# A fused attention and expert kernel: the keys interleaved like the queries, and the next batch's projections put behind its transposes

## What is computed

```python
x = L0_attn_x                                   # 16 sequences, 512 tokens, 128 features
h = _layernorm(x) * (1 + ca) + sa               # sa, ca, ga, sb, cb, gb: rows per sequence
# attention with 16 heads of 8 dimensions and 32 random features per head
q = feature_map(split(h @ Wq.T + bq), orf)      # (exp(y @ orf.T / 8**0.25 - |y|**2 / (2*sqrt(8))) + EPS) / sqrt(32)
k = feature_map(split(h @ Wk.T + bk), orf)
v = split(h @ Wv.T + bv)
kv, ksum = einsum('nlm,nld->nmd', k, v), sum(k, axis=1)
out = (q @ kv) / (q @ ksum)
x = x + ga * (out @ Wo.T + bo)
h = _layernorm(x) * (1 + cb) + sb
# eight experts 128 -> 512 -> 128; every token goes to the one with the largest gate value
x = x + gb * _L0_ffn_ref(h, gate_W, gate_b, W1, b1, W2, b2)
```

## Time and profile before

| what | value |
|---|---|
| median of three runs | 381.62 us |
| span of the profiled execution | 360.6 us |
| TensorE matmul busy | 338.8 us, 94% |
| VectorE, ScalarE, GpSimd busy | 75%, 74%, 59% |
| first stage, q features of batch 1 to those of batch 15 | 29.5 to 204.2 us |
| second stage | from about 211 us to the end |
| granted TensorE clock, mean | 0.998 |

### The profile page before, as it was taken

The page is one execution under the profiler, slowest core; times in us unless marked ns, Lnnn a source line. Parts: engine busy times, 40 slices in busy tenths (PEclk is TensorE's granted clock), DMA queues, the critical chain, the costliest instruction groups (busy, mean ns, idle before and its releaser), DMA issues.

```text
span 360.6 us, 13729 instructions
## 1 busy us (share of the span) xinstructions
PE 338.8 (94%) x4823; PEld 263.9 (73%) x4823; DVE 271.2 (75%) x1104; ACT 265.1 (74%) x644; POOL 213.2 (59%) x262
## 2 busy tenths in 40 slices
PE   6899999899988999998999999999999999999994
PEld 5445765566465566646665669999989999999993
DVE  3456997898879789878887978887677676666653
ACT  2688988799878888977888756676656667666761
POOL 3142386776667757857854618846767455545554
PEclk9999999999999999999999999999999999999999
DMA  7174656774566547444432467445657665545410
GB/s 233 50 253 166 210 184 221 259 243 160 177 227 205 176 167 230 163 132 156 153 133 100 149 163 227 142 118 150 194 161 269 209 184 147 147 128 135 137 38 12
DMA packets 40211, 60.47 MB, mean 168 GB/s; under 512 B 5426, under 2 KB 28086, under 8 KB 40016
## 3 DMA queue, kind: packets, MB, share of 16 engines
q1 hardware_dynamic: 33776, 42.54, 39.9%
q0 software_dynamic: 6368, 17.05, 12.5%
HBM read 28.63 MB, written 19.34 MB: 133 GB/s over the span
## 4 chain that ended last, share of the span: by engine, by line
PE 60%; ACT 15%; DMA 10%; DVE 6%; issue 5%; POOL 1%; SPq 1%; DVEq 1%; POOLq 0%; ACTq 0%
PE ps_proj L1350 16%; PE ps_feat L1337 9%; DMA qmix<-qsqs 9%; PE ps_proj L1132 6%; PE ps_den_gate L1337 4%; PE ps_proj L1182 4%; PE ps_kv L1337 4%; ACT qf L627 3%; ACT qvals L606 2%; ACT shared L588 2%; PE ps_kv L1198 2%; PE ps_out L1330 2%; ACT den L656 2%; ACT shared L581 2%; ACT kvm L600 2%
## 5 line engine op out<-in xcount | busy, mean ns | idle before, releaser
L545 POOL DMA_INDIRECT out<-kf,modb x71 | 70.1, 987 | 52.4 <-DVE kf L1060 47.0
L507 POOL DMA_INDIRECT experts_lists<-pay,slot x64 | 65.9, 1030 | 43.4 <-DVE slot L893 29.5
L1350 PE MATMUL ps_proj<-w2sb,qf 128*128 x568 | 75.0, 275 | 0.4 <-ACT qf L690 0.4
L1350 PEld LDWEIGHTS ps_proj<-w2sb,qf 128*128 128x128 f32 x568 | 68.9, 192 | 0.6 <-issue 0.6
L681 ACT ACTIVATE xT<-ps_out 128x128 f32<-128x128 f32 x71 | 19.7, 277 | 44.8 <-PE ps_out L1330 44.1
L1055 DVE TENSOR_TENSOR kf<-ps_proj,firsts_sb 128x128 f32<-128x128 f32 x71 | 20.7, 291 | 34.6 <-PE ps_proj L1350 22.6
L690 ACT ACTIVATE qf<-ps_feat,shared 128x128 f32<-128x128 f32 x144 | 40.9, 374 | 0.0
L1337 PE MATMUL ps_feat<-xT,shared 128*128 128x128 f32 x288 | 38.8, 277 | 1.5 <-issue 0.9
L1337 PEld LDWEIGHTS ps_feat<-xT,shared 128*128 128x128 f32 x288 | 35.0, 192 | 2.8 <-issue 1.7
L1132 PE MATMUL ps_proj<-shared,wsb 128*128 128x512 f32 x62 | 33.3, 620 | 1.0 <-ACT shared L581 0.4
L977 DVE COPY shared<-firsts_sb 128x516 f32 x71 | 31.4, 442 | 1.6 <-issue 1.5
(11 more groups left out here) (189 smaller groups left out, 890.3 us busy)
## 6 DMA issues: line engine op xcount, KB each, us to landing
modb<-experts_lists SPq DMA_DIRECT2D x71, 196.0 KB, 2.8
xall<-in_x SPq DMA_DIRECT2D x16, 256.0 KB, 3.0
pay<-modb SPq DMA_DIRECT2D x16, 256.0 KB, 3.0
qmix<-qvals SPq DMA_DIRECT2D x30, 128.0 KB
qmix<-qsqs SPq DMA_DIRECT2D x30, 128.0 KB
modb<-modulation_rows SPq DMA_DIRECT2D x4, 768.0 KB, 5.2
firsts_sb<-in_firsts SPq DMA_DIRECT2D x8, 322.0 KB, 4.2
w2sb<-in_w SPq DMA_DIRECT2D x8, 256.0 KB
```

The lines of the kernel that those rows point to most:

```text
L507: g_.indirect_dma_start(out=lists, in_=pay[b.home][:, t, :], in_offset=None, out_offset=bass.IndirectOffsetOnAxis(ap=slot[b.home][:, t:t + ...
L545: g_.indirect_dma_start(out=rows_out, in_=yb[u], in_offset=None, out_offset=bass.IndirectOffsetOnAxis(ap=token, axis=0), bounds_check=last ...
L1350: ins = mm(Y[u % 2][:, 0:D], g[u % R4][:, c * P:(c + 1) * P], w2sb[:, bass.ds(e * DFF + c * D, D)], start=(c == 0), stop=(c == FC - 1))
```

## The change

The key weights get the column order that the query weights have. kvals and ksqs are copied by four DMAs per batch into a new tile kmix (mix_k, ahead of mix_q in SyncE's order), from batch 1 on. The k features of batches 1 to 15 are then one product from kmix with the moving operand feat_q, 64 columns wide, for each of 4 token tiles, 2 halves and 4 row groups: 32 matmuls as before, each with 32 rows and 128 stationary columns. Batch 0 keeps the two-product form with constants in the new order.

On TensorE the k projection of b+1 now stands right behind the transposes that it needs, the q projection right behind the kv product, and the transposes of h2 ahead of the k features. On ScalarE the copies of k come before the copy of kv, and the squares of q right behind the values of q.

```diff
+            def mix_k(v):
+                sp.wait_ge(s_kst, 2 * v + 1)
+                for n in range(2):
+                    sp.dma_start(kmix[n::2, n, :], kvals[n::2, :]).then_inc(s_kmix, 16)
+                sp.wait_ge(s_kst, 2 * v + 2)
+                for n in range(2):
+                    sp.dma_start(kmix[1 - n::2, n, :], ksqs[n::2, :]).then_inc(s_kmix, 16)
             for v in range(1, B):
+                mix_k(v)
                 mix_q(v)
...
                 q_pair(b, 1, first)
-                kvm_copy(b)
                 if not last:
                     k_values(b + 1)
                     k_squares(b + 1)
+                kvm_copy(b)
+                if not last:
                     q_values(b + 1)
+                    q_squares(b + 1)
                 act.wait_ge(s_den, b.v + 1)
...
-                if not last:
-                    q_squares(b + 1)
                 if b.v + 2 < B:
                     normalise1(b + 2)
...
+            def k_features(b):
+                pe.wait_ge(s_kmix, 64 * b.v)
+                pe.wait_ge(s_fq, 1)
+                pe.wait_ge(s_eps, b.v)
+                pe.wait_ge(s_qst, b.v + 1)
+                pe.wait_ge(s_exp, NC * b.v)
+                for t in range(LT):
+                    for n in range(2):
+                        for c in range(NC):
+                            at = slice(c * CW, (c + 1) * CW)
+                            ins = mm(QB[c][:, t * P + n * HP:t * P + (n + 1) * HP], kmix[at, n, t * P:(t + 1) * P],
+                                     feat_q[at, n, :], start=True, stop=True)
...
-                k_features(b, first)
                 if not first and not second:
                     transpose_h2(b + -2, first=third)
+                if first:
+                    first_k_features(b)
+                else:
+                    k_features(b)
...
+                if not last:
+                    project(b + 1, 0)
                 kv_product(b, first)
                 if not last:
-                    project(b + 1, 0)
+                    project(b + 1, 1)
...
                 kv_transpose(b, first)
-                if not last:
-                    project(b + 1, 1)
```

More of the change, by code:

```diff
@@ L80 @@
 R_NORMQ = R_ORFQ + P
-R_NORMV = R_NORMQ + P
-R_END = R_NORMV + P
+R_END = R_NORMQ + P
 class Batch:
@@ L142, in build @@
         feat_q = sb("feat_q", [P, 2, P // 2])
-        feat_v = sb("feat_v", [P, P])
         bv_cols = sb("bv_cols", [P, D])
@@ L172, in build @@
         qsqs = sb("qsqs", [P, L])
+        kmix = sb("kmix", [P, 2, L])
         qmix = sb("qmix", [P, 2, L])
@@ L281, in build @@
         s_qsq = sem("q_squares_ready")
+        s_kmix = sem("k_mix_ready")
         s_qmix = sem("q_mix_ready")
@@ L1141, in v_project, with first_k_features @@
                 ins.then_inc(s_proj, 1)
[L1143 to L1149, removed]
+            def first_k_features(b):
+                pe.wait_ge(s_kst, 2)
                 for t in range(LT):
@@ L1159, in k_features @@
                             ins.then_inc(s_feat, 1)
+            def k_features(b):
[10 more added lines that the diff above has]
+                                     feat_q[at, n, :], start=True, stop=True)
+                            if t == LT - 1 and n == 1:
+                                ins.then_inc(s_feat, 1)
             def q_features(b, first=False):
@@ L1172, in q_features @@
                         at = slice(c * CW, (c + 1) * CW)
-                        mm(QB0[c][:, :], feat_v[at, :], qvals[at, :], start=True, stop=False)
+                        mm(QB0[c][:, :], feat_w[at, :], qvals[at, :], start=True, stop=False)
                     for c in Q_ORDER:
                         at = slice(c * CW, (c + 1) * CW)
-                        mm(QB0[c][:, :], rsb[at, R_NORMV:R_NORMV + P], qsqs[at, :], start=False, stop=True).then_inc(s_feat, 1)
+                        mm(QB0[c][:, :], norm_w[at, :], qsqs[at, :], start=False, stop=True).then_inc(s_feat, 1)
                     return
@@ L1304, in batch @@
                 kv_transpose(b, first)
-                if not last:
-                    project(b + 1, 1)
-                else:
+                if last:
                     keep_busy(14, H)
@@ L1415, in _constants @@
     for r in range(P):
-        head = r // DH % (CW // DH)
-        c[r, C_NORM + head * M:C_NORM + (head + 1) * M] = -1.0 / (2.0 * DH ** 0.5)
+        at = C_NORM + (r % 2) * HP + r % CW // 2 // DH * M
+        c[r, at:at + M] = -1.0 / (2.0 * DH ** 0.5)
     c[:, C_PREF:C_PREF + E] = np.arange(E, 0, -1)
@@ L1437 @@
     w[:, W_O:W_O + D] = a(L0_attn_Wo).T
-    orf = a(L0_attn_orf).T
-    for head in range(NH):
-        at = W_ORF + head % (CW // DH) * M
-        w[head * DH:(head + 1) * DH, at:at + M] = orf
     w[:, W_GATE:W_GATE + E] = a(L0_ffn_gate_W)
@@ L1454 @@
                 rows[square, R_NORMQ + n * HP + j * M:R_NORMQ + n * HP + (j + 1) * M] = -1.0 / (2.0 * DH ** 0.5)
-                rows[value, R_NORMV + n * HP + j * M:R_NORMV + n * HP + (j + 1) * M] = -1.0 / (2.0 * DH ** 0.5)
-    w[:, W_Q:W_Q + P] = w[:, W_Q:W_Q + P][:, source]
-    w[:, W_BIAS + 1] = w[source, W_BIAS + 1]
+    for n in range(2):
+        w[:, n * P:(n + 1) * P] = w[:, n * P:(n + 1) * P][:, source]
+        w[:, W_BIAS + n] = w[source, W_BIAS + n]
+    w[:, W_ORF:W_ORF + P] = rows[:, R_ORFQ:R_ORFQ + P]
     firsts = np.zeros((P, E, WB), np.float32)
```

2 lines of the change are left out of this document (removed).

## The result

The changed kernel takes **434.0 us** (median of five runs, 428.39 to 435.57), the kernel before 383.65 beside it (five runs, 381.19 to 385.29). The ratio is 1.128, with a 95% interval of 1.119 to 1.138. So the medians lie 50 us apart. The forecast was 427, 45 us more, in a range of 410 to 438.

A forecast was written before the change was run, and what follows sets the result against it. TensorE was taken as full in the first stage, every wait a hole. Fourteen periods of 15.41 us add 41.0, batch 1 adds 4: +45 on the span 360.6, plus 21.0 outside it, gives 427 us; range 410 to 438.

The forecast's parts named there:

- First projection, +1.06: TensorE idles 1.12 us for hT at Q (start of a batch's q features)+2.93; kv product follows: +1.06 us per period.
- Second projection, +0.97: Before the first attention product (A), the copy of kv loses its cover, the projection's slot: +0.97 us per period.
- h2, +1.42: Before the k features, TensorE waits 0.92 us for h2; its 0.50 of transposes loses ScalarE's cover: +1.42 per period.
- Shape and one pass, +0.12 and 0: In the k features, one more operand-shape change per batch costs 0.12 us; halving moved columns gains nothing.
- The rival by which moved columns set the pace, 0.18: The k features take 1.0 us less, 15 times: 412 us in all; chance 0.18.
- kmix, 0: Before the k features, four added DMAs per batch are hidden by the h2 wait or up to 0.4 late: 0.
- Its rival, 0.11: kmix lands late and the k features wait 0.4 to 1.3 us past h2: 438 us; chance 0.11.
- qmix: Before the q features, all 8.2 us of TensorE's waits for these transfers go.
- K to next Q, 4.74: From the start of the k features to the next q features: 4.74 us, ended by ScalarE's second exponential.
- Batch 0 to 1, +4: First two holes plus kmix landing late for batch 1's k features: +4 us, ends +2 and +5.
- Clock, 0.03: Rival: TensorE, busy some 77% of a period, loses clock, all its work stretches, time passes 440; chance 0.03.
- Second stage, 0: The 71 expert blocks keep their code and order, so they are costed at nothing.

The follow-up runs named there:

- the first by taking it back: Changed kernel with the kv product back ahead of the first projection: 422.71 us, 1.099 against the kernel before.
- 1.7 alone: Kernel before with only the first projection moved ahead of the kv product: 387.56 us, 1.066.
- the second alone: Kernel before with only the second projection moved ahead of the transpose of kv: 374.06 us, 1.028.
- the order without the h2 wait: Changed kernel with the transposes of h2 back behind the k features: 421.51 us, 1.104 against the kernel before.
- the changed kernel's own order with its holes filled: Changed kernel with 14, 12 and 12 small dummy bf16 matmuls ahead of TensorE's three waits: 432.69 us, 1.126 against the kernel before.
- the two-product kernel: Changed kernel with k features of batches 1 to 15 as two accumulated products of 128 moving columns, without kmix transfers: 434.34 us, 1.130 against the kernel before.

## Why the forecast held, step by step

The mechanism was right: three groups of instructions were moved ahead of what they wait for, on an engine that runs its list in order. The sizes below are read from the changed kernel's trace, in its most common round.

- **First projection, +1.06.** It starts at Q+2.93, as said. The hole is 1.11 (1.12 forecast).
- **Second projection, +0.97.** The hole before A is 0.75 by the trace, and the distance from the transpose of kv to A 1.05, against 1.10 in the earlier trace rows. The two together put A at Q+7.18; the forecast said Q+7.15. How they share it depends on which is undone: 1.23 for the first by taking it back, 1.7 alone, 0.85 for the second alone (undisturbed rounds of 12.7). Alone neither is worth the slot that the forecast charged, as the two hide one another's waits.
- **h2, +1.42.** Transposes at A+3.11 against A+2.9; VectorE's scaling took 1.44 us, where the earlier trace rows has 1.14. So +0.2, mis-sized within the 0.2 that the forecast allowed. Taking it back saves 1.0 to 1.15 a round (15.75 to 14.6 or 14.75), with 0.24 of kmix in its place in one of them. The trace of the kernel before could have told the 0.2: the round of the earlier trace rows is one of five in which the scaling takes 1.14 or 1.15, and in the other nine it takes 1.34 to 1.45, as in this one:

```profile
73.76 1.45 DVE L744 SCALAR_TENSOR_TENSOR pay<-pay,rstd,modb 128x128 f32<-128x128 f32 x4
```

- **Shape and one pass, +0.12 and 0.** Transposes and switch are 0.58 (0.62 forecast); the steps are 0.11 us with 64 moving columns and with 128. The rival by which moved columns set the pace, 0.18, falls. The Trainium skill, "TensorE: Matmul & The Clock Gate", LDWEIGHTS (loading the stationary operand), says that the load goes by the stationary columns; the pair of traces, with 128 of them in both, agrees.
- **kmix, 0.** In the round above the squares' transfers leave the queue at 136.77, Q+8.4 and not Q+7.7, as two issues took 2.43 us. At Q+10.87, behind the transposes of h2, the k features started without a wait for them. Its rival, 0.11, falls for these rounds, and comes true in two rounds and in batch 1 of the order without the h2 wait. For batch 1 see below.
- **qmix.** No wait is left, as said.
- **K to next Q, 4.74.** 4.88 in most rounds, 4.55 where ScalarE's exponential starts at K+2.07. The rows that the forecast took it from, of a faster execution, did not show the 0.3.
- **Batch 0 to 1, +4.** +1.4 between the two traces, below the lower end of +2. But the forecast's reason, kmix landing after its place in batch 1, is seen in all six other traces with kmix: the k features of batch 1 wait 1.05 to 4.47 us for it, 1.86 in the changed kernel's own order with its holes filled. Q of batch 1 comes at 32.7 to 38.9 us in them, not at 32.5, in part by low clocks, since it is 35.6 in the two-product kernel too. The profiled run was the fastest, so what batch 1 costs in the others is not known.
- **Clock, 0.03.** Partly true: 3 rounds of 14 at 0.90, about 3 us in this trace.
- **Second stage, 0.** -1.3 us.

The period was forecast at +2.93 and came out at +3.18; the low clock's 3 us over 14 periods are 0.2 of that difference. Against the traces sizes were off and cancelled: the periods too cheap by 3.6, batch 1 too dear by 2.6, the second stage by 1.3. So the sum's 45 against the traces' 44.7 is luck, and against the medians the forecast is 5 us too low: 427 for 434.0. Where these 5 us lie is open, since the one trace is of the fastest run; late kmix in batch 1 and more rounds at the low clock are what the neighbouring kernels' traces suggest. The step from the span to the time was wrong in itself: the 21.0 us are not a fixed cost outside the span, but the difference between two executions of the kernel before. It did no harm, because the sum was made as a difference.

## What to carry to other kernels

On an engine that runs its list in order, an instruction moved ahead of its operand costs the slots that used to hide the wait; read for each wait what stands between, and price a pair of moves together, since either may cover what the other uncovers. A one-pass form that halves moved columns gains nothing where the step stays the same, 0.11 us here, and its transfers then need a cover of their own. Look for small copies on which a chain hangs before trusting that an earlier start carries through. Read a duration from all rounds of a trace, not from one, and before you match a sum to a trace, see where its run lies among the others.

## What the runs showed of the hardware

- **Scatter and small copy.** In two traces a 128x2 copy of VectorE out of PSUM came at A+0.78 to A+1.27 when GpSimd's issue of an indirect DMA (1.09 us) had started at A-0.28 to A+0.29, in 22 rounds; in a third, on another chip, it came at A+0.38 to A+0.46 under the same issue, in 11. The cause is open.
- **Clock.** In three of 14 rounds where TensorE stood for about 1.1, 0.75 and 1.05 us the granted clock was 0.50 for a few us. In the other eleven it was 1.00, and in all 14 of the two-product kernel, with the same holes. The mean was 0.84 and 0.80 in two rounds with waits of 3.17 and 2.05 us.
- **Executions.** The same kernel before took 363 us on one chip and 383 on two others. Its two traces, with spans of 360.6 and 381.9 us, have mean clocks of 0.998 and 0.985. The difference lay for the most part in ScalarE's late starts: some 12 us of xT waits in the second stage, and 0.1 to 1.2 in front of an exponential in the first. A trace of one and a median of the other must not be subtracted.
